# Query and key stacks of two float32r parts in smaller row tiles, whole maxima turned, and new orders for all queues

## The reference

```python
x = layernorm(x + attn0(x))   # 32 query heads of 8, 8 key/value heads of 8
x = layernorm(x + ffn0(x))    # silu(x@G*gs) * (x@U*us), then @D*ds; 768 wide, weights rounded to float8
x = layernorm(x + attn1(x))   # 16 query heads of 16, 8 key/value heads of 16
x = layernorm(x + ffn1(x))    # the same form, 688 wide, weights lut[idx] from a table of 16 values
```

```python
scores = einsum('bqhd,bkhd->bhqk', xq, keys) / sqrt(DH)
probs = softmax(scores)
context = einsum('bhqk,bkhd->bqhd', probs, values)
```

## Time and profile before

| | |
|---|---|
| median of 3 runs | 378.01 us (377.78 to 379.86) |
| the profiled execution's own time | 376.9 us |
| its span in the profile | 375.1 us |
| busy: PE, DVE, ACT, POOL | 307.7, 262.9, 258.4, 184.1 us |
| mean granted clock of PE | 0.914 |

### The profile page before, as it was taken

How to read it: one execution, slowest core, us unless ns; L and a number is a source line. 1 busy time by engine, 2 the same in 40 slices (tenths; PEclk the granted TensorE clock), 3 DMA queues, 4 the chain that set the end, 5 groups by cost and what they waited for, 6 DMA issues and landing times.

```text
span 375.1 us, 7392 instructions
## 1 busy us (share of the span) xinstructions
PE 307.7 (82%) x2592; PEld 196.2 (52%) x2592; DVE 262.9 (70%) x464; ACT 258.4 (69%) x471; POOL 184.1 (49%) x249
## 2 busy tenths in 40 slices
PE   4853128687878998899979997999999999999991
PEld 3621002232425645455537663665567776789990
DVE  7539789778787899698998978459851775226351
ACT  1776599897778658977978787597767655644440
POOL 4353350401463247813495649573357533367663
PEclk9968555669899999999999999899999999999996
DMA  6984421100311001410010320130057000000000
GB/s 188 319 207 117 122 92 42 58 14 24 107 51 28 0 4 32 113 34 27 2 25 25 86 72 0 44 109 3 2 161 216 15 3 1 2 31 29 2 30 28
DMA packets 24875, 23.09 MB, mean 62 GB/s; under 512 B 3542, under 2 KB 24838, under 8 KB 24838
## 3 DMA queue, kind: packets, MB, share of 16 engines
q1 hardware_dynamic: 24838, 22.61, 21.1%
HBM read 10.47 MB, written 3.26 MB: 37 GB/s over the span
## 4 chain that ended last, share of the span: by engine, by line
PE 38%; DVE 14%; ACT 12%; issue 11%; SPq 11%; POOL 8%; DMA 4%; DVEq 0%; POOLq 0%; ACTq 0%
PE FB L1198 11%; PE FB L1211 6%; ACT PB L810 5%; SPq L517 4%; DVE MX L925 4%; PE MM L1087 4%; DVE LV L1014 4%; PE PV L1142 4%; SPq L524 3%; PE SC L1117 3%; DMA QS<-QP 2%; PE FB L1170 2%; PE SC L1122 2%; DVE HF L976 2%; PE FB L1043 2%
## 5 line engine op out<-in xcount | busy, mean ns | idle before, releaser
L925 DVE TENSOR_REDUCE MX<-MM 128x4 f32<-128x1024 f32 x96 | 117.2, 1221 | 36.3 <-PE MM L1087 30.7
L810 ACT ACTIVATE PB<-SC 128x1024 f32<-128x1024 f32 x96 | 98.1, 1021 | 29.4 <-PE SC L1117 15.4
L1087 PE MATMUL MM<-KS,QS 62*128 62x256 bf16 (+1 forms) x384 | 49.0, 302 | 32.4 <-DVE MX L925 25.2
L1142 PE MATMUL PV<-PB,VP 128*32 128x256 f32 x768 | 64.3, 416 | 0.2 <-ACT PB L810 0.2
L675 POOL TENSOR_TENSOR HL<-HF,HH 128x256 fp32r<-128x256 f32 (+1 forms) x48 | 36.3, 761 | 54.1 <-ACT HH L786 54.0
L1087 PEld LDWEIGHTS MM<-KS,QS 62*128 62x128 bf16 (+1 forms) x384 | 18.9, 98 | 62.1 <-DVE MX L925 40.3
L1014 DVE COPY_PREDICATED LV<-LB,LV 128x432 f32<-128x432 uint8 x70 | 46.8, 729 | 1.4 <-DVE NT L952 0.6
L1198 PE MATMUL FB<-XH,W 128*128 128x256 f32 x192 | 43.7, 309 | 0.5 <-DVEq L979 0.5
L1198 PE MATMUL FB<-XL,W 128*128 128x256 f32 x192 | 38.6, 283 | 1.0 <-POOL XL L648 0.9
L1117 PE MATMUL SC<-QS,KS 64*128 64x256 bf16 x256 | 27.3, 294 | 11.5 <-ACT PB L810 8.9
L693 POOL TENSOR_SCALAR LV<-LB,LD,LT 128x432 f32<-128x432 f32 x40 | 28.2, 717 | 13.8 <-ACT LB L854 13.8
(11 more groups left out here) (93 smaller groups left out, 572.7 us busy)
## 6 DMA issues: line engine op xcount, KB each, us to landing
QS<-QP SPq DMA_DIRECT2D x48, 128.0 KB, 2.4
IX<-in_idx SPq DMA_DIRECT2D x10, 216.0 KB, 2.8
dw<-LO SPq DMA_DIRECT2D x10, 216.0 KB, 1.9
W1L<-dw SPq DMA_DIRECT2D x10, 216.0 KB, 4.0
KS<-KP SPq DMA_DIRECT2D x24, 64.0 KB, 2.0
XT<-in_xt SPq DMA_DIRECT2D x4, 256.0 KB, 2.9
X<-in_x SPq DMA_DIRECT2D x4, 256.0 KB, 5.6
out<-X SPq DMA_DIRECT2D x4, 256.0 KB, 2.1
```

Source lines behind the costliest of these rows:

```text
L810: act.activation(PB[:, quad % PB_QUADS, kt, :, :], SC[:, :, :], ACT.Exp, scale=DH[layer(j)] ** -0.5).then_inc(exp_done, 1)
L925: dve.tensor_reduce(mx, MM[:, :, :].rearrange("p (f i) s -> p f i s", f=2), axis=AX.X, op=ALU.max).then_inc(max_red, 1)
L1087: ins = pe.matmul(MM[:, 2 * f + i, :], QS[lo:lo + r, j % NST, qs + h, qt * P:(qt + 1) * P], keys(j)[lo:lo + r, j % NST, ks, :], start=True ...
L1142: ins = pe.matmul(PV[32 * c:32 * c + 32, r % 2, :], v, PB[:, quad % PB_QUADS, kt, place(j, c), :], start=part == 0, stop=part == (3, 1)[la ...
```

## The change

**Parts.** Queries and keys are split in two parts of float32r, a four-byte type, and three products are stacked (`Q_PART = (0, 0, 1)`, `K_PART = (0, 1, 0)`). `STRIDE` is 4 for both layers: three rows of products for each dimension and one that stays zero, the last of which (row 31 of each 32) holds the maximum. Layer 0's heads take tiles of 32 rows, layer 1's tiles of 64. A unit of products in either layer now consists of pairs in two different row tiles. `qmid`, `kmid`, the second subtraction and `KR` are gone; POOL's `qdif` writes `QP[:,1]` directly; the key difference is taken by DVE from PSUM (new step `kv` on DVE).

**Maxima.** The maxima stay whole (float32r): DVE's two instructions for each `mt` are gone, PE turns `MX` directly with two accumulating products of 256 columns against a shifted identity `IDR`, ACT negates while it copies, and one DMA of 16 rows takes the place of two or one.

**Start.** Eight products of the identity with itself run first on PE; their result is overwritten. DVE clears only job 0's part of `QS` before `stacks_set` reaches 1, POOL clears the rest; each layer 0 weight has its own semaphore. The loads of layer 1's `WQ` and `WK` are each cut into four DMAs that pick groups of 8 or 4 columns.

**Orders.** All five strings are written anew.

```diff
-Q_PART = (0, 0, 0, 1, 1, 2)
-K_PART = (0, 1, 2, 0, 1, 0)
+Q_PART = (0, 0, 1)
+K_PART = (0, 1, 0)
 NPROD = len(Q_PART)
-STRIDE = (8, NPROD)
-STACK = (62, 96)
+STRIDE = NPROD + 1
+TILE = (32, 64)
...
+        def rows_of(j, m, f):
+            lo = 64 * m + 32 * f
+            return slice(lo, lo + TILE[layer(j)])
...
                     else:
-                        sp.dma_start(WQ[1][:, :, :], wq1.rearrange("(t p) n -> p t n", p=P)).then_inc(ld_w1, 16)
-                        sp.dma_start(WK[1][:, :, :], wk1.rearrange("(t p) n -> p t n", p=P)).then_inc(ld_w1, 16)
+                        for t in range(DT):
+                            at = slice(t * P, (t + 1) * P)
+                            for m in range(2):
+                                sp.dma_start(
+                                    WQ[1][:, t, m * P:(m + 1) * P].rearrange("p (d e) -> p d e", d=16),
+                                    wq1[at, :].rearrange("p (d e) -> p d e", d=16)[:, :, 8 * m:8 * m + 8]
+                                ).then_inc(ld_w1, 16)
...
                 elif kind == "qdif":
                     j = step[1]
                     wait_free(pool, ("q", j))
-                    pool.tensor_tensor(QR[:, :], QR[:, :], QP[:, 0, :], ALU.subtract).then_inc(q_dif, 1)
+                    pool.tensor_tensor(QP[:, 1, :], QR[:, :], QP[:, 0, :].bitcast(F32),
+                                       ALU.subtract).then_inc(q_parts, 1)
...
+                elif kind == "kv":
+                    j = step[1]
+                    n = KV[layer(j)] * DH[layer(j)]
+                    dve.wait_ge(k_hi, j + 1)
+                    dve.tensor_tensor(KP[0:n, 1, :], bank[0:n, 0:S], KP[0:n, 0, :].bitcast(F32),
+                                      ALU.subtract).then_inc(k_parts, 1)
...
+            for _ in range(N_EARLY):
+                pe.matmul(SC[:, 0, 0:P], IDN[:, :], IDN[:, :], start=True, stop=True)
...
                     for i in range(2):
                         for f in range(2):
                             if layer(j) == 0:
-                                g, qt, h = 2 * (u // 4) + f, u // 2 % 2, 2 * (u % 2) + i
+                                at, e, g = rows_of(j, x % 2, f), 2 * (x // 2) + i, x // 2
                             else:
-                                g, qt, h = 2 * (u // 2) + f, u % 2, i
-                            lo, ks, qs = stacked(j, g)
-                            ins = pe.matmul(MM[:, 2 * f + i, :],
-                                            QS[lo:lo + r, j % NST, qs + h, qt * P:(qt + 1) * P],
-                                            keys(j)[lo:lo + r, j % NST, ks, :], start=True, stop=True)
+                                at, e, g = rows_of(j, f, 0), 2 * x + i, x
+                            ins = pe.matmul(MM[:, 2 * f + i, :], QS[at, j % NST, e, qt * P:(qt + 1) * P],
+                                            KS[at, j % NST, g, :], start=True, stop=True)
...
                     for qt in range(2):
-                        ins = pe.matmul(bank[0:h, qt * P:(qt + 1) * P],
-                                        MS[:, m % 2, qt, 0:halves(j), :, :].rearrange("q f a h -> q (f a h)"),
-                                        IDB[:, :], start=True, stop=True)
+                        ins = pe.matmul(bank[0:16, 0:S], MX[l][:, j % 2, qt, 16 * p:16 * p + 16],
+                                        IDR[:, (1 - qt) * P:(3 - qt) * P], start=qt == 0, stop=qt == 1)
```

More of the change, by code:

```diff
@@ L350, in two_layer_kernel @@
         ld_xt = [sem(f"ld_xt{i}") for i in range(NXT)]
-        ld_w0 = sem("ld_w0")
+        ld_w0 = [sem(f"ld_w0{i}") for i in range(3)]
         ld_w1 = sem("ld_w1")
+        ld_wo1 = sem("ld_wo1")
         ld_s = sem("ld_s")
@@ L382, in two_layer_kernel @@
         stacks_set = sem("stacks_set")
-        ones_in = [sem(f"ones_in{i}") for i in range(NST)]
+        stacks_zero = sem("stacks_zero")
         q_in = [sem(f"q_in{i}") for i in range(NST)]
@@ L387, in two_layer_kernel @@
         max_red = sem("max_red")
-        m_hi = sem("m_hi")
-        m_split = sem("m_split")
         m_parts = sem("m_parts")
-        m_rows = [sem(f"m_rows{i}") for i in range(2)]
+        m_rows = sem("m_rows")
         score_mm = sem("score_mm")
@@ L430, in wait_free, with qstack_count, kstack_count @@
             eng.wait_ge(fill_free[bank], use + 1)
-        def stack_count(j):
-            return 16 * NPROD * (j // NST + 1)
+        def qstack_count(j):
+            return 16 * 2 * NPROD * (j // NST + 1)
+        def kstack_count(j):
+            return 16 * NPROD * sum(2 - layer(i) for i in range(j % NST, j + 1, NST))
         def xt_count(j):
             return 16 * sum(layer(i) == 0 for i in range(j % NXT, j + 1, NXT))
-        def rows_count(n):
-            return 16 * sum(halves(i // 2) for i in range(n % 2, n + 1, 2))
         def quad0(j):
@@ L460, in rows @@
             return min(P, (I0, I1)[l] - i * P)
-        def stacked(j, g):
-            if layer(j) == 0:
-                return 64 * (g % 2), g // 2, 4 * (g // 2)
-            return 0, g, 2 * g
+        def rows_of(j, m, f):
+            lo = 64 * m + 32 * f
+            return slice(lo, lo + TILE[layer(j)])
         def place(j, c):
@@ L556, in _ @@
                     sp.wait_ge(m_parts, n + 1)
-                    for half in range(halves(j)):
-                        row = 64 * half + STACK[layer(j)]
-                        sp.dma_start(QS[row:row + 2, j % NST, 8 * p:8 * p + 8, :],
-                                     MP[16 * half:16 * half + 16, n % 2, :]).then_inc(m_rows[n % 2], 16)
+                    sp.dma_start(QS[31:P:32, j % NST, 4 * p:4 * p + 4, :].bitcast(F32), MP[:, :].bitcast(F32)).then_inc(m_rows, 16)
                 elif kind == "ldx":
@@ L727, in _ @@
                     if j >= 1:
-                        act.wait_ge(k_in[(j - 1) % NST], stack_count(j - 1))
+                        act.wait_ge(k_in[(j - 1) % NST], kstack_count(j - 1))
                     act.activation(KP[0:nv, 0, :], bank[0:nv, 0:S], ACT.Copy).then_inc(k_hi, 1)
-                    if j >= 1:
-                        act.wait_ge(k_parts, j)
-                    act.activation(KR[0:nv, :], bank[0:nv, 0:S], ACT.Copy).then_inc(fill_free[slot], 1)
-                elif kind == "qmid":
-                    j = step[1]
-                    act.wait_ge(q_dif, j + 1)
-                    act.activation(QP[:, 1, :], QR[:, :], ACT.Copy).then_inc(q_mid, 1)
-                elif kind == "kmid":
-                    j = step[1]
-                    n = KV[layer(j)] * DH[layer(j)]
-                    act.wait_ge(k_dif, j + 1)
-                    act.activation(KP[0:n, 1, :], KR[0:n, :], ACT.Copy).then_inc(k_mid, 1)
                 elif kind == "mt":
                     _, j, p = step
-                    m, h = 2 * j + p, HEADS[layer(j)]
+                    m = 2 * j + p
                     act.wait_ge(mt_ready, m + 1)
-                    if m >= 2:
-                        act.wait_ge(m_rows[m % 2], rows_count(m - 2))
-                    act.activation(MP[0:h, m % 2, :], bank[0:h, 0:S], ACT.Copy).then_inc(m_parts, 1)
+                    if m >= 1:
+                        act.wait_ge(m_rows, 16 * m)
+                    act.activation(MP[:, :], bank[0:16, 0:S], ACT.Copy, scale=-1.0).then_inc(m_parts, 1)
                     act.wait_ge(m_parts, m + 1)
@@ L908, in _ @@
                 kind = step[0]
-                if kind in FILL and kind != "mt":
+                if kind in FILL:
                     slot = fill[step][0]
@@ L926, in _ @@
                                       axis=AX.X, op=ALU.max).then_inc(max_red, 1)
[L927 to L939 removed]
+                elif kind == "kv":
[4 more added lines that the diff above has]
+                                      ALU.subtract).then_inc(k_parts, 1)
+                    dve.wait_ge(k_parts, j + 1)
+                    dve.sem_inc(fill_free[slot], 1)
                 elif kind == "turn":
@@ L1050, in _ @@
                     nv = KV[l] * DH[l]
+                    if l == 0:
+                        pe.wait_ge(ld_w0[1 + part], 16)
                     if part == 1:
@@ L1072, in _ @@
                     if u == 0:
-                        pe.wait_ge(q_in[j % NST], stack_count(j))
-                        pe.wait_ge(k_in[j % NST], stack_count(j))
-                    r = STACK[layer(j)]
-                    m = unit0(j) + u
-                    if m >= 1:
-                        pe.wait_ge(max_red, m)
+                        pe.wait_ge(q_in[j % NST], qstack_count(j))
+                        pe.wait_ge(k_in[j % NST], kstack_count(j))
+                    n = unit0(j) + u
+                    if n >= 1:
+                        pe.wait_ge(max_red, n)
+                    qt, x = u % 2, u // 2
                     for i in range(2):
@@ L1104, in _ @@
                         m = 2 * j + 2 * v // UNITS[layer(j)]
-                        pe.wait_ge(m_rows[m % 2], rows_count(m))
```

(6 more changed lines are left out.)

156 lines of the change are left out of this document (66 added, 90 removed), and 236 rows, old and new, of the table ORDER.

## The result

The changed kernel takes 389.71 us (median of 4 runs, 386.92 to 391.4), the kernel before 378.88 beside it. The ratio is 1.031, with a 95% interval of 1.026 to 1.036. The profiled execution took 386.92 us, with a span of 385.0. The forecast of 372.0 was wrong in its sign, and the range of 360 to 387 missed the time as well.

A forecast was written before the change was run, and what follows sets the result against it. The prediction saw no single bound: PE at the lower clock early, DVE fullest in the middle, PE full from 300 us. Terms -3 - 4 + 4.5 - 2.5 - 1 = -6 from 376.9 gave 370.9, plus 1.1 to the median: 372.0, range 360 to 387.

The forecast's parts named there:

- The third rival: Between 27 and 75 us: full clock gives some 40 units 0.2 us each, 8 us, so 364; chance 0.20.
- Layer 0 products: 4.5 us more: Layer 0 units: 0.10 us exposed load each, half of 14 us counted, less what neighbours absorb; ends 1 and 14.
- the second rival: Both one-buffer loops: all exposed loads on the path, layer 0 costs 14 us plus 2 at lower clock; 383, chance 0.20.
- Layer 1 products: 2.5 less: Layer 1 maxima and scores: parallel pairs save 13.7 us, less 5.6 for loads and 5.5 for tiling changes.
- last stack: 1 less: Job 7's stacks and the rest: one copy, one subtraction and three issues fewer, 1 us less.
- Work removed: 4 less: Instructions dropped on DVE and ACT: 2 us less from each; nothing counted for POOL's 20.
- The start: 3 less: Program start: first maximum 4.4 us earlier, first score hardly earlier because of DVE's queue; 3 us taken, ends 1 and 4.4.
- the first rival: Four-byte loads in neighbouring row tiles don't overlap: 28 us more PE time in layer 0; 391, chance 0.13.
- The short runs: Layer 1's weight transfers ahead of job 1's stack: free until about 50 us; chance a tenth of the second rival's.

The follow-up runs named there:

- the kernel with both edits: Changed kernel with stacks in bfloat16 of two parts and layer 0's maxima and scores in 64-row tiles; 363.5 us, ratio 0.964 to the kernel before.
- the doubled keys: Changed kernel with two-part bfloat16 stacks, layer 0's keys stored twice with the other head's rows zero, 64-row tiles; ratio 1.0006 to the kernel before.
- the control: Changed kernel with only layer 0's exponential taken of a thousandth of the score, 32-row tiles kept; ratio 1.032 to the kernel before.

## Why the prediction was wrong

Of the sum, -3 - 4 + 4.5 - 2.5 - 1, taken one by one:

- **A term that was missing: the clock, 9.3 us.** This is the largest error. The sum took every duration at the clock that the earlier trace rows shows and never asked whether the change would move it. The third rival asked, with the opposite sign ("the clock stays up"). No row of before had products in 32-row tiles; the two runs with tiles of other height show that it is the step from tiles of 64 to tiles of 32 rows that keeps 1.2 GHz on until 110 us, most likely by the rows in use. (The 0.61 and 0.39 of that rival are the products' durations; the reader at 23.38 started 0.64 behind.)
- **"Layer 0 products: 4.5 us more": the step that failed by its mechanism.** The single load was sized right: 0.10 forecast, 0.11 measured (0.43 against 0.32). What failed is "half of the 128 counts, because only half showed a wait". Measured are 2.4 + 8.4 = 10.8 us for 128 units, 0.084 a unit: about three quarters of the 14 that all of them would cost, where the sum took a third (and an upper figure, since it holds all that the format costs). That lies nearer to the second rival, which gave layer 0 14 us and 2 more for the lower clock. In a loop with one buffer the product is late and its reader is then late, also where the profile put no wait down; there are now 55 waits where there were 35.
- **"Layer 1 products: 2.5 less" and "last stack: 1 less": together 9.2 without the loads, and about 6 came.** Behind job 4's first score the kernel with both edits gained 0.3, but the new order also leaves more for then (6 gate or up steps, 3 down steps and 2 of keys or values: 36 products of 0.118 and an estimated 1 us for each of the last two, some 6 us). For the loads 5.6 was forecast and 3.4 measured. The sum also counted the exposed load for the stack's own products alone. The whole-array products behind a change of division pay it as well: between 328.75 and 329.52 a unit and the pair behind it take 0.77, where the sum's own terms (0.22 + 0.09 + 0.10 + 0.24) make 0.65 and the kernel before had 0.68. Some 20 units of layer 1 stand so, which makes about 2 of the 3 us that are missing, by this estimate. Maxima take 0.34 ahead of a score unit and 0.43 ahead of other kinds, where the prediction said 0.24 to 0.34.
- **"Work removed: 4 less": about 8 came** between the marks (13.6 less the 6 us that the order moved out), which I can't split between DVE's and ACT's work and the orders.
- **"The start: 3 less": nothing came.** The first maximum was forecast at 19.6 and came at 20.82, 3.2 us earlier than before; the first exponential was forecast at 54 and came at 59.3. Without the format and the clock it would be 56.1, no better than the 55.8 before. The prediction had seen that DVE's queue decides there, and still took 3.
- **The weights load in parallel**, as the sum had it against the first rival: the starts of the two loads of a pair lie 3 ns apart, and in a layer 0 unit, whose four loads are two such pairs, 0.11 is added once.
- **The short runs** cost nothing, as said, but only because nothing stood close behind them. With the doubled keys, taking them away gave back 6.5 us (0.983 against 1.0006).

Put together, -13.6 in place of -16.2 (the sum without its 4.5 and 5.6 for loads), +14.2 in place of +10.1, and +9.3 in place of nothing: 9.9 us from span to span instead of -6.

The Trainium skill ("TensorE: Matmul & The Clock Gate", section "Weight-path perf modes") says that only loads of a type other than FP32 are sped up. The trace agrees, and counts float32r as FP32: the median load of the maxima takes 186 ns in float32r, 96 in bfloat16. The same page, section "Part 1: The HAM clock gate", says that the clock follows how busy the engine has been. Here the measurement goes further and decides: 19.97 of 20 us busy in 32-row tiles at 0.50, and 16.85 busy in 64-row tiles at 0.78.

## What to carry to other kernels

A change to the shape of TensorE's tiles can change its clock: read the granted clock by window before the durations, and ask of each new shape whether it puts more or less of the array to work. In a loop with one buffer an added 0.11 us on the producer cost up to 0.08 us each time here, though the profile of the kernel before put a wait down for only half of the units. When a unit is given another division of the array, price the load of what stands behind it too. And an issue queue that costs nothing in one order can cost most of its length in the next, so when transfers are added, count what stands behind them.

## What the runs showed of the hardware that was not expected

- TensorE's granted clock stayed at 0.50 through 20 us in which it was busy 19.97 with products of 32 rows; the same stretch with idle products of 128 rows had 0.91. The last of these ran at 53 us, and the clock was back at 0.50 in 60:80.
- Tiles of 64 instead of 32 rows cost nothing in time by themselves (40.4 against 40.5 us from job 3 to job 4, both at 1.00) and raised the clock of 100:120 from 0.75 to 1.00; the control, with the same small values in 32-row tiles, stayed at 0.75.
- A float32r load in a tile of 32 rows takes 181 ns at the least, hardly less than one of the whole array (185 in the earlier trace rows): the height of the tile doesn't shorten it.
- A transfer of layer 1's weights in runs of 16 or 32 bytes takes SyncE 1.2 to 2.1 us to issue (the first of the eight 0.63, all eight 12 us), a plain one 0.43 to 0.47.
